# One causal mask moved from VectorE to TensorE, with a table of shifts for the planner of a fused four-layer kernel

## What is computed

```python
x = x + moe0(x, cond)      # shared gated MLP + top-2 of 8 experts (gelu), sigmoid router
x = x + moe1(x, cond)      # the same with two shared experts
# layer 2, over the positions t in order, h starts as cond:
gate = sigmoid(h @ Wh.T + z_t @ Wz.T + b);  h = tanh(h * (1 - alpha) + gate * z_t)
# layer 3, 16 heads of 8, an image key and value ahead of the 256 words:
scores = q @ k.T / sqrt(8);  scores = where(kj <= qi + 1, scores, -10000)
out = softmax(scores + mask) @ v @ c_proj_w + c_proj_b
```

## Time and profile before

| | us |
|---|---|
| median of 3 runs (439.58 to 440.62) | 439.76 |
| the profiled execution's own time | 439.82 |
| its span, first to last instruction | 437.8 |
| PE busy | 414.9 (95%) |
| PE weight load busy | 306.4 (70%) |
| DVE busy | 291.6 (67%) |
| ACT busy | 249.4 (57%) |

### The profile page before, as it was taken

How to read it: one execution, slowest core, us unless ns; L and a number is a source line. 1 busy time by engine, 2 the same in 40 slices (tenths; PEclk the granted TensorE clock), 3 DMA queues, 4 the chain that set the end, 5 groups by cost and what they waited for, 6 DMA issues and landing times.

```text
span 437.8 us, 13080 instructions
## 1 busy us (share of the span) xinstructions
PE 414.9 (95%) x4568; PEld 306.4 (70%) x4568; DVE 291.6 (67%) x983; ACT 249.4 (57%) x869; POOL 86.2 (20%) x366
## 2 busy tenths in 40 slices
PE   2999999899999999999999999899999999999994
PEld 2777877767777778777566767657765776777772
DVE  5875665877566665666458766447753987996662
ACT  3642664554663664654755447575657555756881
POOL 6320321231231331222322123121111000000000
PEclk9999999999999999999999999999999999999998
DMA  8510000000000000000000000000000100100001
GB/s 299 199 20 9 5 1 1 1 2 1 1 2 1 1 2 2 1 1 1 2 1 0 2 3 3 0 2 4 2 2 3 26 3 6 24 4 4 10 23 25
DMA packets 11222, 7.70 MB, mean 18 GB/s; under 512 B 8983, under 2 KB 10263, under 8 KB 11159
## 3 DMA queue, kind: packets, MB, share of 16 engines
q1 hardware_dynamic: 10727, 6.61, 4.9%
q10 hardware_dynamic: 432, 0.27, 0.2%
HBM read 5.39 MB, written 1.05 MB: 15 GB/s over the span
## 4 chain that ended last, share of the span: by engine, by line
PE 80%; ACT 9%; DVE 7%; issue 2%; DMA 1%; POOL 1%; DVEq 0%; ACTq 0%
PE ybk L1068 18%; PE cbk L1242 12%; PE hid L1221 10%; PE ybk L1193 6%; PE vbk L1221 4%; DVE cbk L1568 3%; PE hid L1119 3%; PE cbk L1246 2%; PE hid L1094 2%; ACT hb L916 2%; PE hid L1169 2%; ACT dd L990 2%; PE hid L1053 2%; PE cbk L1169 2%; ACT hs L995 1%
## 5 line engine op out<-in xcount | busy, mean ns | idle before, releaser
L1568 DVE TENSOR_TENSOR_SCAN cbk<-dd 128x24 f32<-128x24 f32 x256 | 55.6, 217 | 100.3 <-ACT dd L990 96.8
L1242 PEld LDWEIGHTS cbk<-hs,rec 128*128 128x128 f32 x512 | 76.3, 188 | 55.8 <-ACT hs L995 47.3
L1068 PE MATMUL ybk<-hg,down 128*128 128x256 f32 x352 | 100.3, 400 | 0.8 <-DVE hg L1447 0.5
L806 POOL TENSOR_TENSOR dd<-hs,leak 128x8 f32<-128x8 f32 x256 | 55.7, 218 | 229.2 <-ACT hs L995 225.5
L1242 PE MATMUL cbk<-hs,rec 128*128 128x8 f32 x512 | 92.5, 253 | 4.7 <-ACT hs L995 1.8
L995 ACT ACTIVATE hs<-cbk 128x8 f32<-128x8 f32 x256 | 45.3, 177 | 65.6 <-DVE cbk L1568 64.4
L990 ACT ACTIVATE dd<-cbk 128x8 f32<-128x8 f32 x256 | 46.4, 181 | 55.6 <-PE cbk L1242 54.6
L1221 PE MATMUL hid<-xsp,up 128*128 128x256 f16 x486 | 70.9, 277 | 0.4 <-DVE lg L1386 0.3
L1068 PEld LDWEIGHTS ybk<-hg,down 128*128 128x128 f32 x352 | 58.7, 191 | 6.3 <-DVE hg L1447 1.6
L1221 PEld LDWEIGHTS hid<-xsp,up 128*128 128x128 f16 x486 | 46.7, 106 | 8.7 <-issue 0.7
L1447 DVE TENSOR_TENSOR hg<-hb,hid 128x512 f32<-128x512 f32 x50 | 33.5, 676 | 2.6 <-PE hid L1053 2.5
(11 more groups left out here) (235 smaller groups left out, 658.2 us busy)
## 6 DMA issues: line engine op xcount, KB each, us to landing
qz<-up_in SPq DMA_DIRECT2D x3, 512.0 KB, 7.4
out_dram<-silu SPq DMA_DIRECT2D x4, 256.0 KB, 3.1
x<-x_in SPq DMA_DIRECT2D x7, 128.0 KB, 9.4
down<-down_in SPq DMA_DIRECT2D x1, 768.0 KB, 9.6
att<-att_in SPq DMA_DIRECT2D x1, 743.0 KB, 10.7
down<-down_in SPq DMA_DIRECT2D x1, 640.0 KB, 6.1
kp<-mrow SPq DMA_DIRECT2D x32, 4.0 KB
qz<-rows SPq DMA_DIRECT2D x32, 2.0 KB, 1.7
```

Of the source, the lines that this page charges most:

```text
L806: tts(dd[:, t % ZR, 1, :, 2], hs[:, t, :], leak[:, 0:1].broadcast_to([P, B]), ALU.mult).then_inc(decay, 1)
L1068: m = pe.matmul(ybk[l][:, 0:n], D(l, "w2" if shared else "e2", e * f + i), hg[:, hg_of[made] % NHG, i * n:i * n + n], start=first and i == ...
L1242: pe.matmul(cbk[c % 2][:, o:o + B], wh, hs[:, t, :], start=False, stop=True, skip_group_check=True).then_inc(gate_pre, 1)
L1568: nc.vector.tensor_tensor_scan(vps[chunk_of(t) % 2], dd[:, t % ZR, 0].rearrange("p b o -> p (b o)"), dd[:, t % ZR, 1].rearrange("p b o -> ...
```

## The change

Tile 3 joins `CAUSAL_PE`, so that its 16 SC units on DVE go, and each of its 16 diagonal S units gets the mask product of L1174, as for the other tiles. Besides, a table `LATER` shifts the number of a unit, up or down, by the block to which it belongs (`block_of`: one kind, tile or chunk, and pair), with 0 as the least. 244 blocks have an entry, over all stages of the kernel. The table changes no unit's work, only its place in the orders; prices, patience and the other rules of the planner stay as they are.

```diff
-CAUSAL_PE = (0, 1, 2)
+CAUSAL_PE = (0, 1, 2, 3)
...
+LATER = {('A', 0, 0): -1, ('A', 0, 1): -37, ('A', 0, 2): 14, ('A', 0, 3): 11, ('A', 1, 0): -27, ('A', 1, 1): -2,
...
+         ('A', 3, 0): 15, ('A', 3, 1): 46, ('A', 3, 2): 8, ('A', 3, 3): 158, ('AC', 0, 0): -17, ('AC', 0, 1): 38,
...
+         ('K', 1): -27, ('K', 2): 37, ('K', 3): -177, ('M', 0, 0): -248, ('M', 0, 1): -156, ('M', 1, 0): 6,
...
+         ('S', 3, 0): -36, ('S', 3, 1): -36, ('S', 3, 2): -37, ('S', 3, 3): -36, ('SH', 0, 0): -139,
...
+         ('X', 1, 1): -98, ('X', 1, 3): -303, ('X', 2, 0): 603, ('X', 2, 1): 461, ('X', 2, 2): 546, ('X', 2, 3): 790,
...
+def block_of(key):
+
+    k = key[0]
+    if k in ("R", "RT", "RS", "RD", "RC", "RG", "GT"):
+        return "G", key[1], key[2]
+    if k in ("SA", "SB"):
+        return "SH", key[1], key[2]
+    if k == "Y":
+        return key[:4]
+    if k in ("E", "M", "YE", "AC", "X"):
+        return key[:3]
+    if k in ("K", "KP", "Q", "QP", "V"):
+        return k[0], key[1]
+    if k == "X3":
+        return k, key[1] // QT
+    if k in ("MT", "L", "EI"):
+        return "MT", key[1], key[2]
+    if k in ("A", "S", "SC", "AV"):
+        return "S" if k == "SC" else k, key[1], key[2] // 2
+    return key[:1] if k in ("VI", "W") else key[:2]
...
     for n, (key, bank, need) in enumerate(units):
-        needs[key], number[key] = need, n
+        needs[key], number[key] = need, max(0, n + LATER.get(block_of(key), 0))
```

## The result

The changed kernel takes 426.53 us (median of 4 runs, 426.4 to 429.18) against 440.16 for the kernel before beside it: ratio 0.9705, 95% interval 0.9665 to 0.9746, so 13.6 us faster. The forecast was 436.1 with 430.3 as the lower end. The sign was right, the size was not: the forecast's gain of 3.7 us is about a quarter of the measured one.

The account below looks back on a forecast made before the run. PE was taken to bound the tail behind 339.6 us, and the step chain together with a nearly full PE the part ahead. 439.8 + 2.2 (products) - 5.9 (table) = 436.1 us; forecast range 433 to 438.5, whole range 430.3 to 442.0.

Parts of the forecast that it names:

- the term of the table: New unit order fills PE's filler time ahead of the last scan: 0 to 11.7 us gained, 5.9 taken.
- The upper end is 11.7: Most the table could gain: PE time of the 109 fillers from 200 to 340 us.
- The product's term: 16 mask products on PE in tile 3's stage: +2.2 us, between 0 and +3.4.
- The gap ahead of X: PE's free 0.31 us per pair of batches before X in tile 3's stage, which the mask products would close.
- The pair arithmetic of 0.86 less 0.40: Per pair of tile 3's batches, mask products add 0.86 us on PE; 0.40 free hides some in three of four pairs.
- What the additions cost on DVE: Taking 16 additions (10.8 us) from DVE in the tail: 0 on the path, at most 0.8 us gained.
- X of tile 2 as PE's fill: X of tile 2, set back 461 to 790 places, becomes what PE takes when nothing else is ready; 0.94 us units.
- No gain from shorter steps: Recurrence steps ahead of 339.6 us: up to 12.5 us shorter, but work returns in the full tail; counted 0.
- none at the end: From the last AV to the last O and store: a serial run without additions, unchanged, 0.
- No return: Rival: mask products land on full PE and the table fills nothing; 442.0 us, at most 443.2; chance 0.22.
- The product is free: Rival: the 16 products lie in PE's gaps and the addition's 0.8 us wait is saved; 433.1 us; chance 0.08.
- Nearly all fillers go: Rival: the table replaces the full 11.7 us of fillers with real units; 430.3 us; chance 0.14.

Follow-up runs that it names:

- the wide fillers: Kernel before with DENSE 0.86 instead of 0.62, so 337 fillers and not 149: 445.75 us against 440.44, ratio 1.012.
- a second set: Changed kernel with each of tile 3's 16 mask products done twice, order untouched: 430.79 us, 4.3 more than the changed kernel.
- table only: Changed kernel without the mask product for tile 3, so DVE's additions stay and the table is kept: 424.65 us, ratio 0.9635 to before.
- product-only kernel: Changed kernel with the table emptied, so only tile 3's mask products are added to the kernel before: 444.97 us, ratio 1.0105 to before.
- two halves by kind: Changed kernel with only the table's MoE, recurrence-chunk and load entries, 438.58 us, or only its attention entries, 434.77 us.

## Why the prediction was wrong

**The step that failed** is the term of the table, "I take half, 5.9 us", and behind it "The upper end is 11.7". The mechanism stood: real units went into PE's free time ahead of the last step and left the tail. The size of the free time was wrong twice. It was counted by fillers, which pad a step only to 0.62 us, so that what is free above that had no row; the wide fillers showed some 14.9 us there, and of the 16.1 us that the table moved only 7.8 took the place of fillers. And it was counted from 200 us on, though the fillers go back to 54 us (149 of them, 16.0 us). With 31 us of room the same "half" would have been 15.5 us, and 439.8 + 2.2 - 15.5 = 426.5; that the half is exact to the digit is chance, since nothing but a choice stood behind it. It could have been read: a step takes 1.11 us at the least and its own products keep PE for 0.24 (from 333.64 to the filler at 333.88), so that a step with 0.62 us of work has another 0.25 to spare. In PE's timeline of the kernel before such steps stand one after the other:

```profile
333.64 0.39 PE L1242 MATMUL cbk<-hs,rec 128*128 128x8 f32 x2
333.88 0.38 PE L1246 MATMUL cbk<-id 128*128 128x256 f16 x2
334.13 0.60 PE L1094 MATMUL vbk<-kq,spread 128*128 128x512 f16 x2
334.76 0.39 PE L1242 MATMUL cbk<-hs,rec 128*128 128x8 f32 x2
```

Nor was a choice needed for this term. The table acts only through the planner, and the planner's own end of the plan goes from 423.8 to 408.6 us with the whole change, 15.2 earlier. Taken off 439.8 that gives 424.6, within 2 us of what was measured. The forecast took the planner's prices to be near the rows and didn't use what they add up to.

**The product's term**, +2.2 with +3.4 as its end, had the sign and was too small: +4.6 alone, +4.3 for a second set, +1.9 in the table's order (changed against table only); counted behind the last scan alone, 2.8, 3.6 and 2.7. The gap ahead of X closed as said, and the slot is 0.21 to 0.22. The pair arithmetic of 0.86 less 0.40 fits the profiled execution (+2.4 in the span) and not the runs.

**What the additions cost on DVE**: not isolated. No run has neither additions nor products. With the additions kept and the table in place the kernel is 1.9 us faster, so that they cost less than the products; a second set of products cost 4.3 us where the exchange gave back 1.9, which leaves room for a price of the additions of up to 2.4 us in the table's order. Without the table no relief shows (+4.6).

**X of tile 2 as PE's fill**: wrong. None of these units stands ahead of the last step in either kernel, and without the four entries the difference is within the intervals.

**No gain from shorter steps, none at the end**: right. The last scan came 0.9 us later. The end lost 0.95 us to the clock in the profiled execution, which no step foresaw.

**What was to be seen**: no L1535 rows and no exponential from `hb` to `hb`, 64 mask products, all so. The fillers went to 76 and not "near 95", and the tail from 94.8 to 80.8 us (340.3 to 421.1) and not to 91.

**The rivals.** "No return" had the sign of the kernel without the table, with too low a price (442.0 us, at most 443.2, against 444.97 measured), and was wrong for this one. "The product is free" is refuted by the product-only kernel and by the one that does the products twice. The Trainium skill (Perfetto Trace Analysis, section Identifying the Most-Contended Engine) judges TensorE's headroom by LDWEIGHTS busy time and, beside it, by MFU, the share of the peak arithmetic, which the forecast left out. The first doesn't hold here: the loader's 71% was no headroom where the slots add up to 92%. "Nearly all fillers go", 430.3 us, was nearest and still short, since it had the fillers for the whole room.

## What to carry to other kernels

Count an engine's free time from start to start over whole periods, and not by a marker that the program itself puts into only a part of it; a filler with a threshold hides what lies above the threshold. On a kernel whose first engine is full behind a serial chain and partly free beside it, moving work across the end of the chain can be worth far more than a cheaper unit: here a change that adds 3.4 us of work still came with a gain of 14. Before forecasting what a new order brings, ask the program that makes the order where it ends by its own prices. A table of shifts doesn't scale, since half of each shift lost the gain, though its two halves by kind nearly added up; try it also without the change that came with it, which here was the better version.

## What the runs showed of the hardware

At the end of the changed kernel the granted clock was 0.50, and one product pair took 2.06 us and not 1.11; the kernel before, with the same idle times ahead of that pair, ran it in 1.11. In the table-only profile it fell to 0.83 over 10 us behind two gaps of PE of 0.7 and 0.8 us, while the changed kernel, with the same list of instructions up to there, kept 1.00 in its profile, with a gap of 1.1 us. Leaving out all fillers took the mean clock from 0.996 to 0.97 and cost 3.8 us; adding 55 to 56 to a dense order cost 3.5 us. In the kernel before, 149 fillers beat both none and 337; no other count was tried on it.
